# A decoder on one core: sixteen products of constants at the end of the PE program of five token stages

## What is computed

```
x = layernorm(x + attention(x))              # 16 heads of 16; layer 0 with a position bias, half of the heads
                                             # look back and half look ahead; layer 1 without a mask
x = layernorm(x + cross_attention(x, ctx))   # layer 0 clips the scores
x = layernorm(x + experts(x))                # 8 experts, the best 2 for each token
```

## Time and profile before

| | us |
|---|---|
| median of 3 runs | 2250.22 |
| lowest and highest run | 2247.93, 2252.23 |
| the profiled execution | 2248.09 |
| its span, first to last instruction | 2246.3 |
| mean granted PE clock over the span | 0.921 |

### The profile page before, as it was taken

How to read it: one execution, slowest core, us unless ns; L and a number is a source line. 1 busy time by engine, 2 the same in 40 slices (tenths; PEclk the granted TensorE clock), 3 DMA queues, 4 the chain that set the end, 5 groups by cost and what they waited for, 6 DMA issues and landing times.

```text
span 2246.3 us, 32863 instructions
## 1 busy us (share of the span) xinstructions
PE 1953.8 (87%) x10990; PEld 1007.3 (45%) x10991; DVE 1293.8 (58%) x2318; ACT 994.6 (44%) x1919; POOL 491.3 (22%) x801
## 2 busy tenths in 40 slices
PE   8799999688499999948999999978887999967992
PEld 4344445334466666623222222254443444455661
DVE  3578874786522222256788888456576878562115
ACT  3156665476111111122666666734532666622331
POOL 3311102421132222112200000033151101043440
PEclk9699999799699999978899999988997999978996
DMA  8433313321810000036111130053135333061123
GB/s 232 122 61 60 48 18 72 86 45 52 315 47 30 31 30 30 26 117 142 30 29 29 30 49 9 1 142 59 38 73 109 53 53 58 2 188 45 63 65 122
DMA packets 111607, 157.90 MB, mean 70 GB/s; under 512 B 31543, under 2 KB 88695, under 8 KB 108535
## 3 DMA queue, kind: packets, MB, share of 16 engines
q1 hardware_dynamic: 103986, 135.75, 26.4%
q0 software_dynamic: 7488, 20.46, 2.8%
HBM read 110.44 MB, written 44.72 MB: 69 GB/s over the span
## 4 chain that ended last, share of the span: by engine, by line
PE 65%; DVE 10%; issue 9%; POOL 4%; DMA 4%; SPq 3%; ACT 3%; POOLq 1%; DVEq 0%; ACTq 0%
PE psum L1513 11%; PE psum L1471 11%; PE psum L2129 11%; PE psum L1495 9%; PE psum L2148 7%; PE psum L1026 3%; DVE arena L1587 3%; PE psum L995 3%; PE psum L2139 2%; DMA q_halves<-arena 1%; PE psum L1498 1%; PE psum L1528 1%; POOLq L2376 1%; ACT arena L1554 1%; DVE arena L1081 1%
## 5 line engine op out<-in xcount | busy, mean ns | idle before, releaser
L1554 ACT ACTIVATE arena<-psum 128x512 f32<-128x512 f32 (+1 forms) x1120 | 573.7, 589 | 367.7 <-PE psum L1495 183.2
L1587 DVE TENSOR_REDUCE arena<-psum 128x1 f32<-128x1024 f32 (+3 forms) x352 | 400.1, 1172 | 93.3 <-PE psum L1471 63.5
L1471 PE MATMUL psum<-arena 96*128 96x512 bf16 (+7 forms) x1280 | 366.8, 370 | 35.1 <-DVE arena L1630 17.0
L1495 PE MATMUL psum<-arena 99*128 99x512 bf16 (+7 forms) x1280 | 365.8, 353 | 11.6 <-ACT arena L1554 6.7
L1513 PE MATMUL psum<-arena 128*32 128x512 f32 (+3 forms) x2560 | 281.4, 538 | 1.0 <-ACT arena L1554 1.0
L1573 DVE CUSTOM_DVE_ANT_0 arena<-psum,arena 128x640 bf16<-128x640 f32 (+3 forms) x256 | 250.1, 1021 | 55.8 <-PE psum L1471 54.5
L2129 PE MATMUL psum<-arena 128*128 x780 | 269.8, 493 | 1.7 <-ACT arena L2183 1.1
L1471 PEld LDWEIGHTS psum<-arena 96*128 96x128 bf16 (+1 forms) x1280 | 100.6, 100 | 278.3 <-issue 82.7
L1495 PEld LDWEIGHTS psum<-arena 99*128 99x128 bf16 (+1 forms) x1280 | 123.8, 98 | 184.8 <-ACT arena L1554 76.2
L2233 DVE COPY arena<-psum 128x640 f32<-128x640 f32 (+1 forms) x78 | 59.2, 758 | 253.3 <-PE psum L2139 253.3
L2148 PE MATMUL psum<-arena 128*128 (+1 forms) x780 | 189.0, 384 | 2.1 <-DVE arena L2236 1.2
(11 more groups left out here) (205 smaller groups left out, 2391.4 us busy)
## 6 DMA issues: line engine op xcount, KB each, us to landing
arena<-k_parts SPq DMA_DIRECT2D x144, 128.0 KB
q_halves<-arena SPq DMA_DIRECT2D x80, 192.0 KB, 3.1
arena<-q_halves SPq DMA_DIRECT2D x40, 384.0 KB, 4.8
arena<-q_halves SPq DMA_DIRECT2D x40, 256.0 KB, 5.3
k_parts<-arena SPq DMA_DIRECT2D x48, 192.0 KB, 3.3
arena<-in_L_ffn_w SPq DMA_DIRECT2D x9, 1024.0 KB, 11.8
arena<-y_rows SPq DMA_DIRECT2D x32, 256.0 KB, 4.3
arena<-in_L_ffn_w SPq DMA_DIRECT2D x8, 704.0 KB, 9.1
```

The lines of the kernel that those rows point to most:

```text
L1471: last = nc.tensor.matmul(dst[:, base + lo:base + hi], q[0:rows, qh, h, qb % 4 * P:qb % 4 * P + P], k[0:rows, h, key0 + lo:key0 + hi], sta ...
L1495: last = nc.tensor.matmul(b[:, at0:at0 + width], kk[0:rows, h, kb * P:kb * P + P], q[0:rows, qh, h, c0:c1], start=True, stop=diag is None)
L1554: nc.scalar.activation(probs[k % 4][:, heads[0]:heads[-1] + 1, c0:c1], bank[st_bank[no % 3]][:, 0:len(heads) * width].rearrange("p (h q) - ...
L1587: nc.vector.tensor_reduce(dst, src, AX.X, ALU.max).then_inc(t("taken"), 1)
```

## The change

At the end of the PE program of a token stage that has a `following`, after its last product and before PE drains, sixteen products are added. The stationary operand is `identb`, the moving one 512 columns of bf16 that lie over `ident`, `identb` and `mask_right` (256 words from the start of the constants), and the result goes to bank 4 in t0 and to bank 0 elsewhere. Nobody reads it. In t1, t4 and t5 PE first waits until ACT has copied out the last transposed attention rows of the stage; in t0 until the results of all units have been taken; in t3 there is no wait. That makes 80 products in the program.

```diff
@@ -463,6 +463,7 @@
         pick_max = take(P // 2).bitcast(BF16)
+        steady = arena[:, top[0] - 512:top[0] - 256].bitcast(BF16)
         minus_clamp = take(1)
@@ -1061,6 +1062,13 @@
                     elif kind == "cvalue":
                         context.pe_values(pe, n)
+                if following:
+                    if source == "proj":
+                        pe.wait_ge(t("att"), n_pairs)
+                    elif context:
+                        pe.wait_ge(t("work_free"), len(units))
+                    for n in range(16):
+                        nc.tensor.matmul(bank[4 if context else 0][:, :], identb, steady, start=True, stop=True)
```

## The result

The changed kernel is slower. The first comparison gave 2262.18 us (2255.95 to 2263.60, 4 runs) against 2249.07 (2246.19 to 2252.23, 4 runs), a ratio of 1.0053 with the 95% interval 1.0029 to 1.0076. The forecast was 2249 and the range ended at 2256. Two more comparisons with more runs gave less: 1.0007 (0.9991 to 1.0023; 10 and 31 runs) and 1.0025 (1.0014 to 1.0036; 12 and 35 runs). By the means the changed kernel is 11.8, 2.6 and 5.7 us above the kernel before in the three comparisons. Over all its 26 runs it has a mean of 2257.9 us. The kernel before has 2252.4 over 115 runs of six comparisons, and these reach from 2240.9 to 2260.3 (13 to 14 us within each of the larger comparisons). The change costs about 5 us, 0.2%. Three of the first four runs are over 2261.8 us and only one of the 22 later ones is.

A forecast was written before the change was run, and what follows sets the result against it. It took PE and its clock as what to watch. Zero for at0, xa0, at1, xa1 and the hidden products, -1.3 us for mla, gave 2246.8 from 2248.09; with the runs' median 2.1 us higher, 2249 us, range 2243 to 2256.

The forecast's parts named there:

- The cost at the five places: Ends of t0, t1, t3, t4, t5: sixteen products take 3.5 us at full clock, all hidden by SP's stores.
- The clock: Attention openings: at0, xa0, xa1 open at half clock as before; at1 and mla open at full, losing it before scores.
- The gain of 1.3 us in mla: Opening of mla: at full clock DVE's three waits for PE shrink by 0.55 + 0.51 + 0.26 = 1.3 us.
- Rival (a): All five openings: the clock holds through, halving PE's chain part, 8.5 to 17 us gained, time 2238; chance 0.13.
- Rival (b): Ends of t3 and t5: products run at half clock and outlast SP, costing 5.1 us, time 2255; chance 0.10.
- Rival (c): Gap before mla: the clock is lost there too and nothing changes, time 2250; chance 0.17.
- 0 (xa0): Stage xa0: its remaining gap of 4.6 us still takes the clock, so it opens at half clock and gains nothing.

The follow-up runs named there:

- e3: The changed kernel run again unaltered, against the kernel before: mean 2256.0 us over 10 runs, ratio 1.0007.
- h1: The changed kernel run once more unaltered, against the kernel before: mean 2258.4 us over 12 runs, ratio 1.0025.
- g1: The changed kernel with 32 products in t0, t1 and t4, 16 in t3, 20 in t5: mean 2255.2 us, ratio 1.0012 against the kernel before.
- e1: The kernel before with the sixteen products only at the end of t1: mean 2257.1 us, ratio 1.0019 against the kernel before.
- f2: The changed kernel plus four products before PE's wait for moved maxima in xa0's jobs from the third on: mean 2255.6 us, ratio 1.0015 against the kernel before.
- e2: The changed kernel without the products at t1, keeping those at t0, t3, t4 and t5: mean 2251.3 us, ratio 0.9993 against the kernel before.
- s2: Only the first four stages, sixteen products at the end of t0 alone: mean 559.4 us; without products 561.5 and 562.4 us.
- s3: Only the first four stages, sixteen products at the end of t1 alone: mean 564.6 us; without products 561.5 and 562.4 us.
- s6: Only the first four stages, sixteen products at the end of t1, run again: mean 562.3 us; without products 561.5 and 562.4 us.

## Why the prediction was wrong

**The cost at the five places: right.** 3.6 us for sixteen (forecast 3.5), in each of the five places done before SP; t3 with 0.5 us to spare (0.3). The idle times left came out at 4.15, 4.49, 0.81, 4.72 and 1.31 us for 4.2, 4.6, 0.6, 4.6 and 1.7.

**The clock: right. The gain of 1.3 us in mla: wrong.** at0 opened at half clock, xa0 got the half level within its first rows, at1 and mla opened at full clock and lost it before their scores. The three waits of mla became 0.84, 0 and 0 (forecast 0.7, 0 and 0). But the term -1.3 took DVE's waits for the wait that ends last. The scores also wait for the moved maxima. These were issued 1.6 us sooner and landed 0.5 us later, PE waited 1.99 us for them, and the scores began 0.3 us later than before, counted from the start of the stage. In e3 and h1 PE waited 1.14 and 2.06 us there. mla as a whole is 265.1 us against 264.5.

**Rival (a): its price was the wrong estimate.** Half of PE's share of the chain per stretch (8.5 to 17 us) was taken as the yield of a full clock. g1, with the idle times closed to about 1 us, had the full clock at the first products of all five, and its maxima came 0.2 to 1.6 us sooner. In xa0 DVE stood right behind PE and 0.24 us came back. In at0 and mla 1.6 us came back and went again, since the moves landed no sooner. PE's share of the chain left out both: an engine that another one follows closely, and a transfer that ends the wait anyway.

**Rival (b): did not happen.** No place outlasted SP. That its price of 2255 us is near the 2257.9 of all runs is luck.

**Rival (c): right in its outcome only.** The clock was not lost in mla's gap, and nothing was gained there all the same.

**The step that failed** is the term "0 (xa0)", with the sentence that no transfer is added or moved. The runs show 8 to 10 us more in xa0 in its place, in all three profiles of the changed kernel. Instructions are themselves fetched by transfers: the profile has a queue of kind "instruction" whose packets of 16 KB took 0.9 to 1.4 us around this place. In the kernel before one such packet comes 48.7 us into xa0; in the changed one it comes at 44.3 to 46.9, and there it delays the 4 KB move that PE is about to wait for. PE's wait of 1.2 to 1.8 us is followed by a fall of the clock, and there are six or seven falls to the end of xa0 in place of two. Five of the nine traces with 16 or more products at t1 are hit, those three among them; five ninths of 8.5 us is 4.7, an estimate that is near the measured 5 for the change and 3.7 for t1 alone.

Of this chain these links are shown: the late landing or issue, PE's wait, the fall right behind it and five or more falls after it, in five traces of five and in no other. That the packet is what delays the move is shown by the held transfers, which run when the packet ends, in all five; no kernel was run in which the packet alone was moved. That the cost of 5 us in the mean is this one alone is not shown: e1 is 3.7 us slower with an xa0 of 147.5 us in its one trace, f2 and h1 differ by less than two standard errors, and the shortened kernels show no difference in their means.

Why the packet comes sooner is open. One account is that PE's program has grown: sixteen products with their weight loads are 32 more PE instructions. The count of PE records that have started when it comes (2606 to 2626 in the eighteen traces) does not decide it, as it varies by 20, which is more than the sixteen products added. Two things speak against this account alone. In e2 and s2, with sixteen products at t0, the packet comes at 48.9 and 49.5, as without any. And s3 and s6 are the same kernel, with the packet at 49.7 and at 46.7. A kernel with 32 instructions more and no products was not run.

**The range was too narrow** for a second reason. It took the spread of three runs, 2248 to 2252, as that of the kernel, and reached past it only for the rivals. 115 runs reach from 2241 to 2260. The standard deviation of the runs is 3 to 4 us in both kernels, so a difference of two means of four runs has a standard error of about 2.6 us, and says little on 0.2%.

The page of the Trainium skill cited ahead, "TensorE: Matmul & The Clock Gate" ("HAM oscillation — how this bites in real kernels"), describes a kernel that loses the clock again in every turn of its loop because a short burst is followed by a wait. The trace agrees in part: xa0 in the changed kernel does this in every second job, every 17.1 us, after one late transfer. The rule was read for the gap that the change fills, and it bore on the loop far behind it.

## What to carry to other kernels

Work put into a gap that costs nothing there can still go with a cost elsewhere. The fetches of instructions use the same transfer engines as small moves that an engine waits for, and here one such meeting was followed by 8 to 10 us. Before a gap is filled to keep the clock, follow the stage behind it to its first wait that ends last: if another engine sets the pace there, or a transfer that lands when it lands, the full clock is worth tenths of a us or nothing. And where runs of one kernel spread over 0.6% in one comparison, take the spread from many runs before setting a range, and look at the stages in question in many traces.

## What the runs showed of the hardware

The last transfer of a 4 KB move ended 0.8 us after the end of its issue in fourteen traces, and 1.74 to 1.90 us after it in four in which a 16 KB packet of instructions (1.0 to 1.2 us) fell into it. Two of the move's 32 transfers were held until the packet ended. Once SP's issue of three moves took 2.97 us in place of 1.77 beside such a packet.

Moves that are issued sooner need not land sooner. In the opening of mla three moves of 4 KB behind loads on the same queue took a median of 4.3 us to land in place of 2.3, when they were issued 1.6 us earlier.

A loop can fall in step with the clock's falls: in five executions of xa0 they came every 17.1 us, one for each pair of jobs, from the fifth job to the last ones (in e3 with one step missing), while pairs without a fall took mostly 15 to 16.5 us. Each fall later than 30 us into xa0 went with 1.75 us more.

The highest mean clock among the profiles of whole kernels (0.929, g1, mean time 2255.2 us) and the lowest times did not go together between kernels, though they do between runs of one whole kernel (correlation -0.57 to -0.93).
